# Decoder layer on one core: cross-attention's first batches prepared inside self-attention, layer-norm roots computed on VectorE

## What is computed

```
x = x + self_attention(layernorm(x))    # 32 heads of 8, 8 key heads; compressed, block-selected and window branch, gated
x = x + cross_attention(layernorm(x))   # q = layernorm(x), k = v = ctx_2048; 8 heads of 16
                                        #   (the 128 tokens are the feature axis: softmax over 256 columns)
x = x + moe(layernorm(x))               # 64 experts, 8 chosen, width 64, and one shared expert
layernorm(x) = (x - mean) / sqrt(var + 1e-5)
```

## Time and profile before

| | us |
|---|---|
| median of 3 runs | 1217.5 (1216.9 to 1219.61) |
| profiled execution, its own time | 1218.7 |
| its span | 1216.9 |
| busy in the span: PE / DVE / ACT / POOL | 1095.8 / 606.6 / 566.1 / 621.2 |

### The profile page before, as it was taken

The page is one execution under the profiler, slowest core; times in us unless marked ns, Lnnn a source line. Parts: engine busy times, 40 slices in busy tenths (PEclk is TensorE's granted clock), DMA queues, the critical chain, the costliest instruction groups (busy, mean ns, idle before and its releaser), DMA issues.

```text
span 1216.9 us, 22759 instructions
## 1 busy us (share of the span) xinstructions
PE 1095.8 (90%) x7471; PEld 898.7 (74%) x7504; DVE 606.6 (50%) x1342; ACT 566.1 (47%) x1185; POOL 621.2 (51%) x755
## 2 busy tenths in 40 slices
PE   5969999999999838989767999999999999999996
PEld 3747777776767626666456888888887888888886
DVE  5756777777777547777471332233233322332232
ACT  3426666666666516776543333333332333333332
POOL 3765656565665142210004666666665666566663
PEclk8968999999999958999858999999999999999998
DMA  5201101010101046663005344344344334344341
GB/s 127 62 1 27 28 24 30 22 29 24 28 25 28 18 100 152 144 142 92 1 14 133 99 115 114 97 121 108 103 121 126 105 107 121 98 113 116 96 119 56
DMA packets 74961, 96.92 MB, mean 80 GB/s; under 512 B 20412, under 2 KB 55868, under 8 KB 74892
## 3 DMA queue, kind: packets, MB, share of 16 engines
q1 hardware_dynamic: 74892, 96.05, 30.3%
HBM read 82.73 MB, written 13.12 MB: 79 GB/s over the span
## 4 chain that ended last, share of the span: by engine, by line
PE 57%; DVE 3%; issue 3%; ACT 1%; DMA 1%; POOL 0%; SPq 0%; POOLq 0%; DVEq 0%; ACTq 0%
PE bank L1608 29%; PE bank L1620 15%; PE bank L1277 3%; PE bank L1263 3%; PE bank L1309 3%; DVE xmax L1408 1%; PE bank L1320 1%; PE bank L1288 1%; DMA comb<-combine_scratch 0%; DVE X L1820 0%; PE bank L1295 0%; PE bank L1326 0%; DVE keys_x L1437 0%; PE bank L1583 0%; PE bank L1593 0%
## 5 line engine op out<-in xcount | busy, mean ns | idle before, releaser
L1834 POOL TENSOR_TENSOR hidden<-act_u,comb 128x512 f32<-128x512 f32 x132 | 217.7, 1649 | 215.0 <-DVE act_u L1802 143.9
L1802 DVE TENSOR_TENSOR act_u<-act_g,bank 128x512 f32<-128x512 f32 x132 | 90.8, 688 | 394.0 <-PE bank L1608 365.4
L1708 ACT ACTIVATE act_g<-bank 128x512 f32<-128x512 f32 x132 | 78.9, 598 | 356.6 <-PE bank L1608 356.6
L1608 PE MATMUL bank<-x_hi,up_hi 128*128 128x512 f32 x528 | 209.2, 396 | 5.8 <-POOL up_lo L1839 5.8
L1608 PE MATMUL bank<-x_lo,up_hi 128*128 128x512 f32 x528 | 208.3, 394 | 0.0
L1608 PE MATMUL bank<-x_hi,up_lo 128*128 128x512 f32 x528 | 206.6, 391 | 0.0
L833 ACT ACTIVATE probs<-bank 128x512 f32<-128x512 f32 x192 | 113.8, 604 | 81.9 <-PE bank L656 45.1
L1620 PE MATMUL bank<-down_hi,h_hi 128*128 128x256 f32 x528 | 149.3, 283 | 1.8 <-POOL down_lo L1844 1.8
L1620 PE MATMUL bank<-down_hi,h_lo 128*128 128x256 f32 x528 | 150.0, 284 | 0.0
L1620 PE MATMUL bank<-down_lo,h_hi 128*128 128x256 f32 x528 | 149.9, 284 | 0.0
L1839 POOL TENSOR_TENSOR up_lo<-up_in,up_hi 128x512 fp32r<-128x512 f32 x66 | 85.0, 1288 | 87.6 <-ACT up_hi L1720 87.6
(11 more groups left out here) (258 smaller groups left out, 2180.9 us busy)
## 6 DMA issues: line engine op xcount, KB each, us to landing
comb<-combine_scratch SPq DMA_DIRECT2D x132, 256.0 KB, 3.8
up_in<-in_w_up SPq DMA_DIRECT2D x66, 256.0 KB, 3.5
down_in<-in_w_down SPq DMA_DIRECT2D x66, 128.0 KB, 3.7
keys_x<-key_rows_x SPq DMA_DIRECT2D x32, 192.0 KB, 3.3
key_rows_x<-ctx_hi SPq DMA_DIRECT2D x256, 16.0 KB, 1.5
query_x<-xq_rows_hi SPq DMA_DIRECT2D x64, 64.0 KB, 3.2
ctx_in<-in_ctx SPq DMA_DIRECT2D x16, 128.0 KB, 2.1
key_rows_x<-ctx_lo SPq DMA_DIRECT2D x128, 16.0 KB, 1.5
```

What stands on the lines that cost most here:

```text
L1608: last = nc.tensor.matmul(out[:], wp[p][:, c, s, :], xp[:, c, t:t + 512], start=k == 0, stop=k == 5)
L1708: nc.scalar.activation(act_g[h][:], GATE[h][:], ACT.Silu).then_inc(S(f"gated{h}"), 1)
L1802: nc.vector.tensor_tensor(act_u[h][:], act_g[h][:], UP[h][:], ALU.mult).then_inc(S(f"upped{h}"), 1)
L1834: nc.gpsimd.tensor_tensor(hidden[h][:], act_u[h][:], comb[p][:, 512 * h:512 * h + 512], ALU.mult)\
```

## The change

1. **Layer norm.** `ln_stats_vector` is split into `ln_open` (the seven operations up to `var_eps`) and `ln_close`. ACT's `Ln` and `Exp` are gone; `ln_close` is 11 DVE operations, each behind a wait for the one before: a shift and a multiply-add on the bits as int32, then three Newton steps of three operations. The turns are now 0-3, 4-7, 8-15 (projection), 0-11 and 12-15 (cross-attention), 0-15 (experts). In the projection batch 4 can be normalised once turn 2 is closed; turn 3 is closed at `b == 3` of the loop. Turn 4 is opened in round 12 and closed in round 13 of self-attention; turn 5 is closed at step 2 of cross-attention.
2. **Start of self-attention.** `ck` uses banks 4 and 7, `cv` bank 0. PE runs `query_transposes(0)` and `raw_transposes(0)` between the matmuls of `ck` and those of `cv`. DVE's memsets for `attn_zeroed` stand at the head of `comp_vector`, and the `cv` part moves behind `comp_in(0)`.
3. **Start of cross-attention.** Tiles are placed so that `query_x` covers `proj` and `keys_x` covers `ck`, `ck_sum` and part of `cv`. POOL zeroes `query_x` after its last self-attention work (waiting for `rawT_done` of 16), then makes `xq` of batches 0 to 3. DVE sets `keys_x` 0 to 2 and 3 in round 15. ACT makes `xq_hi` of batches 0 and 1 at units 9 and 11 of round 15, and of 2 and 3 in round 16. SP loads the keys of batches 0 and 1 first. The eight `max_scores` of batch 0 are spread over units 0, 2, 5 and 9 of round 16, ahead of the end of batch 15 on PE; those of batch 1 follow directly. The steps start at 0.
4. **Order within a cross step.** `shift_transposes(i+1)` moves from `u == 0` to `u == 2`, `keep_shift(i+1)` on ACT from `u == 0` to `u == 3`, `xq_hi` from `u == 2` to `u == 0`. `xbias` is gone; `xq_hi` is a copy of `xq`.

```diff
+        def ln_close(dve, n):
+            new = slice(*LN_TURNS[n - 1])
+            chain, past = S("ln_newton"), (n - 1) * 10
+            v, r, t = var_eps[:, new], rstd[:, new], newton[:, new]
+            dve.wait_ge(S("ln_var"), n)
+            nc.vector.tensor_scalar(r.bitcast(I32), v.bitcast(I32), 1, None, ALU.logical_shift_right).then_inc(chain, 1)
+            dve.wait_ge(chain, past + 1)
+            nc.vector.tensor_scalar(r.bitcast(I32), r.bitcast(I32), -1, ROOT_GUESS, ALU.mult, ALU.add).then_inc(chain, 1)
+            for k in range(3):
...
+            ln_open(dve, 2)
             normal(2)
             for b in range(8, 12):
                 batch_stats(b)
             normal(3)
+            ln_close(dve, 2)
+            normal(4)
             for b in range(12, B):
                 batch_stats(b)
-            ln_stats_vector(dve, 2)
+            ln_open(dve, 3)
...
+            query_transposes(pe, 0)
+            raw_transposes(pe, 0)
             pe.wait_ge(S("hid_kept"), 8)
...
+                    if b == B and u in (0, 2, 5, 9):
+                        for m in {0: (0, 1), 2: (2, 3), 5: (4, 5), 9: (6, 7)}[u]:
+                            cross_max_scores(pe, 0, m)
...
+                    if b == B - 1 and u in (9, 11):
+                        cross_query_high(act, (u - 9) // 2)
+                    if b == B and u in (0, 7):
+                        cross_query_high(act, 2 + u // 7)
...
+            cross_zero_queries(pool)
+            for b in range(4):
+                cross_query(pool, b)
+                if b:
+                    cross_query_low(pool, b - 1)
...
+            shift_transposes(0)
+            for u in range(XH):
+                cross_max_scores(pe, 1, u)
...
-                    if u == 0 and 0 <= i + 1 < B:
+                    if u == 2 and i + 1 < B:
                         shift_transposes(i + 1)
...
-                    if u == 0 and 0 <= i + 1 < B:
+                    if u == 3 and i + 1 < B:
                         keep_shift(i + 1)
-                    if u == 2 and 0 <= i + 4 < B:
-                        query_high(i + 4)
+                    if u == 0 and i + 4 < B:
+                        cross_query_high(act, i + 4)
```

More of the change, by code:

```diff
@@ L213, in ln_stats_vector, with ln_open @@
         def ln_stats_vector(dve, n):
+            ln_open(dve, n)
+            ln_close(dve, n)
+        def ln_open(dve, n):
             lo, hi = LN_TURNS[n - 1]
@@ L230, in ln_stats_vector @@
                 .then_inc(S("ln_var"), 1)
[L231 to L239, removed]
-            dve.wait_ge(S("ln_done"), n)
[L242 to L247, removed]
+        def ln_close(dve, n):
[7 more added lines that the diff above has]
+            for k in range(3):
+                dve.wait_ge(chain, past + 3 * k + 2)
+                nc.vector.tensor_tensor(t, r, r, ALU.mult).then_inc(chain, 1)
+                dve.wait_ge(chain, past + 3 * k + 3)
+                nc.vector.scalar_tensor_tensor(t, t, -0.5, v, ALU.mult, ALU.mult).then_inc(chain, 1)
+                dve.wait_ge(chain, past + 3 * k + 4)
+                nc.vector.scalar_tensor_tensor(r, t, 1.5, r, ALU.add, ALU.mult).then_inc(chain if k < 2 else S("ln_done"), 1)
+            dve.wait_ge(S("ln_done"), n)
         def normalise(out, b):
@@ L299, in proj_vector @@
             for b in range(B):
-                if b + 4 < B:
+                if b == 3:
+                    ln_close(dve, 3)
+                if b and b + 4 < B:
                     normal(b + 4)
@@ L639, in score @@
                 if u == 0:
+                    if b == 0:
+                        pe.wait_ge(S("attn_zeroed"), 2)
+                        pe.wait_ge(S("cv_ready"), 1)
                     pe.wait_ge(S("rows_w_kept"), b + 1)
@@ L1249, in cross_loads, with cross_max_scores @@
                         sp.wait_ge(S("xscore_done"), XH * (b - 3))
-                    load_keys(b, p, s)
+                    if b == 3:
+                        sp.wait_ge(S("keys_zeroed"), 2)
+                    if b >= 2:
+                        load_keys(b, p, s)
                     sp.wait_ge(S(f"xq_out{p}"), 32 * (b // 2 + 1))
                     load_queries(b, p, s)
+        def cross_max_scores(pe, b, m):
+            s, c, pair = b % 4, m // 4, MAX_ORDER[m % 4]
+            if b == 0 and m == 0:
+                for n in range(2):
+                    pe.wait_ge(S(f"smax_read{n}"), 4 * B)
+            if m == 0:
+                pe.wait_ge(S(f"ld_heads{b % 2}"), 128 * (b // 2 + 1))
+            if 4 * b + m // 2:
+                pe.wait_ge(S(f"xmax_read{m % 2}"), 4 * b + m // 2)
+            for n in range(2):
+                k = 2 * (pair % 2) + n
+                last = nc.tensor.matmul(XMAX[m % 2][:, n * D:n * D + D],
+                                        query_x[s][0:XROWS, k, pair // 2, c * 128:c * 128 + 128],
+                                        keys_x[s][0:XROWS, k, :], start=True, stop=True)
+            last.then_inc(S("xmax_scored"), 1)
@@ new lines, in cross_query, with cross_query_low @@
+        def cross_query(pool, b):
+            if b >= 2:
+                pool.wait_ge(S("xq_lo_ready"), b - 1)
+            pool.wait_ge(S("ln_done"), 4 if b < 12 else 5)
+            nc.gpsimd.tensor_scalar(xq[b % 2], X[:, b, :], mean[:, b:b + 1], rstd[:, b:b + 1], ALU.subtract, ALU.mult)\
+                .then_inc(S("xq_ready"), 1)
+        def cross_query_low(pool, b):
+            p = b % 2
+            if b >= 2:
+                pool.wait_ge(S(f"xq_out{p}"), 32 * (b // 2))
+            else:
+                pool.wait_ge(S(f"ctx_out{p}"), 384 * (B // 2))
+            pool.wait_ge(S("xq_ready"), b + 1)
+            pool.wait_ge(S("xq_hi_ready"), b + 1)
+            nc.gpsimd.tensor_tensor(xq_lo[p][:], xq[p], xq_hi[p][:], ALU.subtract).then_inc(S("xq_lo_ready"), 1)
@@ L1255, in cross_tensor, with cross_zero_queries, cross_ones @@
+        def cross_zero_queries(pool):
+            pool.wait_ge(S("rawT_done"), B)
+            for s in range(4):
+                last = nc.gpsimd.memset(query_x[s][:].bitcast(F32), 0.0)
+            last.then_inc(S("query_zeroed"), 1)
+        def cross_ones(dve, slots):
+            for s in slots:
+                last = nc.vector.memset(keys_x[s][:].bitcast(F32), 1.0)
+            last.then_inc(S("keys_zeroed"), 1)
         def cross_tensor(pe):
@@ L1434, in cross_vector @@
             for p in range(2):
-                nc.vector.memset(xvalue[p][:, :, :, XC:XC + 1], 1.0)
-            for s in range(4):
-                last = nc.vector.memset(keys_x[s][:].bitcast(F32), 1.0)
-            last.then_inc(S("cross_zeroed"), 1)
-            ln_stats_vector(dve, 3)
-            nc.vector.scalar_tensor_tensor(xbias[:], mean[:], -1.0, rstd[:], ALU.mult, ALU.mult)\
-                .then_inc(S("xbias_ready"), 1)
-            for i in STEPS:
+                last = nc.vector.memset(xvalue[p][:, :, :, XC:XC + 1], 1.0)
+            last.then_inc(S("xvalue_set"), 1)
+            for u in range(XH):
+                cross_reduce_max(dve, 1, u)
+            ln_open(dve, 5)
+            for i in range(B + 2):
+                if i == 2:
+                    ln_close(dve, 5)
                 for u in range(XH):
-                    if 0 <= i + 2 < B:
-                        reduce_max(i + 2, u)
+                    if i + 2 < B:
+                        cross_reduce_max(dve, i + 2, u)
                     if u == 2 and 0 <= i - 2 < B:
```

250 lines of the change are left out of this document (120 added, 130 removed).

## The result

| | median, us | lowest to highest, us | ratio to the kernel before, 95% interval |
|---|---|---|---|
| before | 1217.5 | 1215.4 to 1219.6 (6) | |
| after | 1211.9 | 1207.9 to 1213.0 (6) | 0.9950 (0.9937 to 0.9963) |
| after, a second series | 1212.6 | 1210.4 to 1214.5 (7) | 0.9962 (0.9948 to 0.9976) |

Each ratio is to executions of the kernel before from the same series (their median was 1217.1 in the second). The change makes the kernel some 5 us faster (6.1 and 4.6 by the two ratios, 5.4 by the traces), where I had forecast 21 and a range of 1187 to 1205.

What follows compares the result with a forecast made beforehand. PE, busy 90% of the span, was taken as the bound, with losses where it waits or runs at half clock. Terms -4.3 - 4.2 + 0.2 - 14.8 + 0.8 + 1.6 - 0.3 = -21.0 gave a 1196.5 us median, range 1187 to 1205.

Steps and rivals of the forecast that it cites:

- Within the steps: Cross-attention steps: the reordering removes one PE wait but adds others, netting +0.06 us a step, +0.8 over 14 steps.
- `ln_close(5)`, +1.6: Step 2 of cross-attention: 2.3 us of DVE work ahead of the reductions, partly covered by PE's banks, costs 1.6 us.
- The first two stages: Projection and start of self-attention: shorter waits and less half-clock time gain 4.3 and 4.2 us.
- only the waits: Rival: projection and self-attention's start gain only their waits, clock low as before, 2.3 and 2.4 us; 1200 us, chance 0.10.
- The hand-over: Between self- and cross-attention: the largest term, first cross score at 446.2 instead of 461.0, gaining 14.8 us.
- Half the hand-over: Rival: first loads land later or reductions run one after the other, gain 8 for 14.8; 1203 us, chance 0.13.
- rounds 12 and 13: Self-attention rounds with ln_open(4) and ln_close(4) on DVE ahead of add_branch: cost 0.2 us, bounds 0 and 2.3.
- The experts' norm: Experts: ln_close(6) replaces ACT operations, a table load and Newton operations, 2.6 by 2.3 us: -0.3.
- POOL's memsets beside the maxima: Hand-over: POOL's memsets beside DVE's maxima of batch 15 cost 0, bound 3.6 us.
- The step's wait is really gone: Rival: in cross-attention steps ctx_transposes finds its shift kept, giving -9 us and no +0.8; 1187 us, chance 0.11.
- The shift never missed its score: Slower rival: in cross-attention steps the shift's DMA lands too late for its score; 1225 us at 5 us landing, chance 0.03.
- the wait of 0.7 us: Sign of being right: in each cross-attention step PE waits 0.7 us on ACT's xshift, with period 8.4 to 8.5.

Runs made afterwards that it cites:

- run 11: The kernel before with only the layer-norm part of the change put in (turns cut to five, new projection order): 1214.8 us, ratio 0.9979.
- run 12: The kernel before, unaltered, profiled again in one execution: 1219.0 us.
- run 2: Changed kernel with the old order inside a cross-attention step (shift_transposes and keep_shift at unit 0, xq_hi at unit 2): 1201.8 us, ratio 0.9872.
- run 4: Changed kernel with ctx_transposes moved from unit 3 to 4 and keep_values from unit 4 to 5: 1196.3 us, ratio 0.9831.
- run 3: Changed kernel with ln_close(5) split into three parts behind the reductions of units 3, 4 and 5 of step 2: 1208.0 us, ratio 0.9926.
- run 6: Changed kernel with the keys of cross batch 1 loaded later, at b == 1 in the loop instead of ahead of it: 1211.6 us, ratio 0.9947.
- run 5: Changed kernel with all maxima of cross batch 0 placed behind the end of batch 15, on PE and DVE: 1210.2 us, ratio 0.9931.
- run 9: Changed kernel with the edits of run 3, run 4 and run 5, plus the residual behind the reduction of unit 7: 1190.1 us, ratio 0.9768.
- run 7: Changed kernel with run 6's edit, xq_hi(0) at unit 5 of round 15, both query halves written ahead of the key loads: 1209.1 us, ratio 0.9928.

## Why the prediction was wrong, step by step

The account, from marks in the traces. Eleven traces share the changed first stages (runs 11 and 12 don't), five the changed hand-over, five the changed steps with the block in step 2.

| stretch | before (2 traces) | changed: mean (lowest to highest) | gain | forecast |
|---|---|---|---|---|
| start to A | 422.1 | 417.1 (414.2 to 419.1) | 5.0 | 8.3 |
| A to F | 39.4 | 26.3 (25.9 to 26.7) | 13.1 | 14.8 |
| F to the last cross score | 127.9 | 140.9 (139.3 to 142.1) | -13.0 | -2.4 |
| last cross score to the end | 627.7 | 627.4 (626.7 to 628.1) | 0.3 | 0.3 |
| sum | | | 5.4 | 21.0 |

- **The failed step is "Within the steps", +0.06 us a step.** It was +0.56. Of my terms, the wait at `ctx_transposes` cost 0.95 for 0.71 (start to start from the maxima of unit 3, 1.19 for 0.24): I had taken PE's arrival 0.16 too late, at the chain's mark (531.56) and not at the start in PE's own timeline (531.40), and left out the 0.14 from the kept shift to PE's start. The other terms gave back 0.43 for 0.65: unit 0 became 1.02 shorter (1.37 us from the start of its score to that of its maxima before, 0.35 after), since the wait of 0.84 did go and the transposes with it, and the maxima of unit 1 did wait about as forecast (0.29 for 0.35), but the moved transposes cost the stream 0.21 at unit 2 and `turn_values` 0.10, where I had let them shrink. The rest is 0.04. Each error is under 0.25 us; times fourteen steps they are 7. The old order gave 8.41 (run 2), and without the wait at `ctx_transposes` the new one gave 7.92 (run 4), so this part is shown.
- **Second, `ln_close(5)`, +1.6.** In the old order that is what it costs (1.2 to 1.6 us, run 2). In the new one it costs 4.7 (140.9 from F to the last score against 136.2 in run 3): PE waits 2.10 instead of 0.95, because the block takes 2.9 instead of 2.16 (POOL works beside it; in run 2 POOL's next operation starts at 464.91, after the block has ended at 464.01) and PE reaches the maxima of unit 2 1.55 us after its start instead of 1.96; and the lower clock follows the longer wait. I had costed the two edits each against the step of before; the order cost 8.3 alone (136.2 in run 3 against 127.9 before), the block 1.6 alone (129.5 in run 2), and both 13.0. The single runs are one trace each, and the five traces with both differ by 2.8 among themselves, so the 3 or so that neither has alone is rough.
- **The first two stages**, right in the first trace (8.2 us at the last raw transposes), gave 5.0 at A on average. Waits and starts moved as said (batch 7 at 28.9; POOL 11.9 us earlier). DVE's first `reduce_max`, by which the forecast has its 8.5 us, comes only 7.2 to 7.4 earlier in the two traces of the changed kernel and 5.9 on average: in the five traces with the earliest (75.9 to 76.9) the clock of 66 to 86 us is 0.62 or 0.63, in the six others (77.7 to 79.2) 0.50 to 0.53. Then, from the second raw transposes to the fourth, it is 45.1 to 45.2 us in exactly the four traces in which the clock of 105 to 115 us is 0.83 (runs 2, 5, 6 and 9), 42.4 to 43.5 in the seven in which it is 1.00, and 43.4 before. The rival "only the waits" comes close in number, 4.7, and in part in kind: in 66 to 86 us the clock is no higher than before (0.60), but in 85 to 95 us it is 0.62 to 0.85 for 0.50.
- **The hand-over**: 13.1 for 14.8. Shape and order as worked out, one wait of 6.5 us on the queries' DMA for the "some 5" that I gave. What I missed is the write of the second half, held up by the keys' loads (run 6): from its issue to the first maxima it is 8.1 us (413.24 to 421.30), where I took 6.3. "Half the hand-over" falls.
- **Right**: rounds 12 and 13 (0.2) cost nothing that shows: from the fourth raw transposes to the last it is 251.3 us in both traces of the changed kernel and 251.6 in both of before. The experts' norm (0.3): PE's wait for its first `xn` 5.24 for 5.55. POOL's memsets beside the maxima: `finemax` 0.43 and `rows` 0.18 under a memset of 7.04 us, 0.42 and 0.18 in before. The Trainium skill (SBUF — State Buffer, Who interferes with whom) has it that DVE with two SBUF inputs isn't held by an instruction that only writes SBUF; these rows agree. By the same rule it is held by one that reads: L248 in `ln_close(5)`, two SBUF inputs, took 0.64 us for 0.16 and ended with POOL's `xq_lo` (457.23, 0.73 us; shown as `ctx_lo` in the trace); but four operations of that kind beside POOL's next one (458.07, 1.22 us) took 0.42 and three times 0.16, so the rule gives only part of it.
- **The other rivals.** "The step's wait is really gone" falls: PE waits 0.79 us at L1395 in every steady step. The shift never missed its score: no wait on its DMA stands in a step of the changed kernel. Of my signs, the wait of 0.7 us was there, and the period of 8.4 to 8.5 that should have come with it was not.
- What sets the time at which the clock comes back in the first rounds stays open; no run tells it.

## What to carry to other kernels

An instruction moved out of a wait keeps its own cost, and every instruction behind it on both engines has a new neighbour: write the new step out start to start for each engine, and check the sum against the old period, before it is multiplied by the number of steps. Two edits in one loop are costed together, since the slack that hides the one may be what the other takes. Where a queue of in-order work holds both the end of one stage and the first, DMA-bound piece of the next, the end goes first, or the transfer starts earlier; either was worth 4 to 5 us of that stretch here, and some 3 us of the whole by the ratios.

## What the runs showed of the hardware that I had not expected

- After PE had waited 2.1 us in step 2, with a granted clock of 1.00 in the 6.5 us ahead of it, the clock fell to its lower level (L1409 1.94 for 1.07 us) for some 3 us in the first trace and 7 in the second. It fell in all six traces in which PE waited 1.93 to 2.18 us there (both of the changed kernel and runs 4 to 7); with a wait of 0.95 us at the same place (run 2, one trace) it did not fall (1.00 in that stretch).
- The same program up to self-attention gave a clock between 0.62 and 0.85 in one stretch of 10 us, and A between 414.2 and 419.1.
- A 128 KB write took 3.4 to 4.4 us (eight traces) to be seen by its issuer with 768 KB of loads just ahead of it in the queue, 2.8 with 384 KB (one trace), and 1.9 with none (two traces).
